# A second attention layer with split keys: one transposed set for both parts of the keys, two copies of the high part, and the maxima one step earlier

## The reference, cut to what matters

```python
ss_g = ss * ms                                   # sigmoid gates, only the 3 largest of 5 kept
sd_g = sd * md
q5 = (x @ Wq).reshape(b, t, H, E, DH)
kv = (x @ Wkv).reshape(b, t, 2, H, E, DH)
k5, v5 = (kv[:, :, 0], kv[:, :, 1])
q = jnp.einsum('bthed,bthe->bhtd', q5, sd_g)
k = jnp.einsum('bthed,bthe->bhtd', k5, ss_g)
v = jnp.einsum('bthed,bthe->bhtd', v5, ss_g)
attn = jax.nn.softmax(jnp.einsum('bhid,bhjd->bhij', q * scale, k), axis=-1)
out = jnp.einsum('bhij,bhjd->bihd', attn, v)
o5 = jnp.einsum('bthd,dm->bthm', out, Wo).reshape(b, t, H, E, DIM)
return jnp.einsum('bthem,bthe->btm', o5, md)
```

## Time and profile before

| | |
|---|---|
| runs | 1804.98 us median of 3 (1800.93 to 1805.13) |
| profiled execution | 1798.95 us, of it span 1797.1 us |
| TensorE matmul | 88% of the span busy |
| VectorE | 72% |
| ScalarE | 53% |
| GpSimd | 41% |
| granted TensorE clock, mean | 0.957 of full speed |

### The profile page before, as it was taken

One profiled execution on the slowest core, in us unless ns is written; L12 is line 12 of the kernel. 1 busy time (PEld: TensorE's weight loads), 2 busy tenths in 40 slices (PEclk: granted clock), 3 DMA queues, 4 the chain that ended last, 5 costly groups with the idle time before them and its releaser, 6 DMA issues.

```text
span 1797.1 us, 26827 instructions
## 1 busy us (share of the span) xinstructions
PE 1582.9 (88%) x8612; PEld 998.3 (56%) x8612; DVE 1292.7 (72%) x2371; ACT 945.1 (53%) x1582; POOL 743.5 (41%) x690
## 2 busy tenths in 40 slices
PE   3799999999999952579999999998999999999997
PEld 2455555555555452556656566565665565665554
DVE  4996785785788357967777777777677777777763
ACT  3456657657555601155655655655656546555552
POOL 2610000000000003647668667488486576685312
PEclk9899999999999975799999999999999999999997
DMA  2000000000000000000000000000000000000000
GB/s 60 1 1 1 1 1 1 1 1 1 1 1 1 1 12 0 12 11 1 1 12 1 5 8 1 12 1 1 12 1 1 12 1 1 1 1 1 1 10 15
DMA packets 12227, 9.38 MB, mean 5 GB/s; under 512 B 3840, under 2 KB 11584, under 8 KB 12096
## 3 DMA queue, kind: packets, MB, share of 16 engines
q1 hardware_dynamic: 12096, 7.66, 1.6%
HBM read 6.61 MB, written 1.05 MB: 4 GB/s over the span
## 4 chain that ended last, share of the span: by engine, by line
PE 64%; POOL 13%; DVE 13%; issue 5%; ACT 3%; SPq 0%; DMA 0%; DVEq 0%; ACTq 0%; POOLq 0%
PE ps L810 10%; PE ps L627 8%; PE ps L644 7%; PE ps L659 7%; POOL z L1432 5%; PE ps L800 4%; PE ps L785 4%; PE ps L801 4%; PE ps L602 4%; POOL onm L1428 3%; PE ps L768 2%; POOL gs L1405 2%; DVE mxp L1111 2%; PE ps L821 2%; PE ps L770 2%
## 5 line engine op out<-in xcount | busy, mean ns | idle before, releaser
L1111 DVE TENSOR_REDUCE mxp<-ps 128x1 f32<-128x512 f32 (+3 forms) x560 | 354.0, 670 | 109.8 <-PE ps L627 55.8
L997 ACT ACTIVATE pbuf<-ps 128x512 f32<-128x512 f32 x512 | 301.5, 598 | 205.5 <-PE ps L801 201.9
L899 ACT ACTIVATE pbuf<-ps 128x1024 f32<-128x1024 f32 (+3 forms) x320 | 281.8, 897 | 197.0 <-PE ps L644 98.0
L1315 DVE TENSOR_TENSOR den<-den,pbuf 128x1024 f32<-128x1024 f32 x224 | 354.1, 1581 | 2.6
L627 PE MATMUL ps<-kM,qT 128*128 128x512 f32 (+3 forms) x640 | 243.1, 425 | 8.9 <-ACT kM L886 4.0
L1268 DVE TENSOR_TENSOR gt<-ps,gate 128x320 f32<-128x320 f32 x384 | 177.3, 484 | 100.8 <-PE ps L770 67.3
L810 PE MATMUL ps<-pbuf,h_v 128*64 128x512 f32 x1024 | 249.7, 608 | 0.0
L1288 DVE CUSTOM_DVE_ANT_0 relu<-ps,relu 128x512 f32<-128x512 f32 x256 | 174.1, 683 | 81.3 <-PE ps L785 78.9
L800 PE MATMUL ps<-q1T,k1T 128*128 128x512 f32 x512 | 212.4, 415 | 10.1 <-ACT pbuf L997 6.2
L644 PE MATMUL ps<-qT,kM 128*128 128x512 f32 (+3 forms) x640 | 207.2, 398 | 8.4 <-ACT pbuf L899 8.4
L983 ACT ACTIVATE relu<-ps 128x512 f32<-128x512 f32 x256 | 151.8, 596 | 107.8 <-PE ps L785 83.6
(11 more groups left out here) (215 smaller groups left out, 2746.3 us busy)
## 6 DMA issues: line engine op xcount, KB each, us to landing
wraw<-in_Wkv SPq DMA_DIRECT2D x16, 160.0 KB, 2.4
wraw<-in_Wq SPq DMA_DIRECT2D x8, 160.0 KB, 2.2
out<-x SPq DMA_DIRECT2D x4, 256.0 KB, 3.1
...
```

The lines of the kernel that those rows point to most:

```text
L899: nc.scalar.activation(pbuf0[:, u % NP0, :, off:CH], ps[:, b:b + 2, off:CH], ACT.Exp, scale=float(D0) ** -0.5).then_inc(s_exp, 1)
L997: nc.scalar.activation(pbuf1[:, u % NP1, i, :], ps[:, i, :], ACT.Exp, scale=float(D1) ** -0.5).then_inc(s_exp1, 1)
L1111: v.tensor_reduce(mxp[:, i, h:h + n, b], ps[:, ring0.bank(step), 0:w * n].rearrange("p (h k) -> p h k", h=n), AX.X, ALU.max).then_inc(s_re ...
L1315: v.tensor_tensor(dn, dn, w, ALU.add).then_inc(s_den1, 1)
```

## The change

1. `hi` writes the high part of the keys once, into columns 0 to 63 of sk1; `lo` writes the low part into columns 64 to 127; sk2 is gone.
2. There are two sets of transposes a chunk instead of three: w=0 turns sk1 (high rows above low rows), w=1 is the queries' set. The w=1 set of the low keys, its turn in the ring of banks and its wait are gone.
3. The copies: from the w=0 bank ScalarE makes three copies of 64 rows (k1T rows 0 to 63, k1T rows 64 to 127 from the same high rows, k2T from the low rows), the last of them releasing the bank; from the queries' bank two as before. Five copies a chunk instead of four.
4. MAX1 is 2.6 instead of 1.6, and q2 stands 2 after m instead of 1: m(c) and all dif and max steps stand one unit earlier, q2(c) stays where it was. The dif and max of chunk 0 have 4.3 units instead of 5.3.

```diff
@@ -53,7 +53,7 @@
 MAX0 = (-1.5, 6.0, 21.0, 44.0)
 PROJ1 = (2.05, 20.5)
 STAGE1 = (2.2, 3.0, 3.7)
-MAX1 = 1.6
+MAX1 = 2.6
 
 
 def preparation0():
@@ -103,7 +103,7 @@
         for c in range(NC):
             end = start + step * TPC * (c + 1)
             out += [(end + STAGE1[0], ("hi", h, c)), (end + STAGE1[1], ("lo", h, c))]
-            out += [(end + STAGE1[2] + 0.3 * w, ("t", h, c, w)) for w in range(3)]
+            out += [(end + STAGE1[2] + 0.3 * w, ("t", h, c, w)) for w in range(2)]
             if c % 2:
                 out.append((end + STAGE1[2] + 0.65, ("kd", h, c // 2)))
         for c in range(NC):
@@ -115,7 +115,7 @@
                 items += [("dif", *b)] if b else []
                 items.append(("max", *a))
             out += [(start + (end - start) * k / len(items), item) for k, item in enumerate(items)]
-            out += [(end, ("m", h, c)), (end + 1, ("q2", h, c))]
+            out += [(end, ("m", h, c)), (end + 2, ("q2", h, c))]
     return sorted(out, key=lambda p: p[0])
 
 
@@ -290,7 +290,6 @@
         mxp1 = s1("mxp1", [P, TPC, NC // 2])
         mx1 = s1("mx1", [P, TPC])
         sk1 = s1("sk1", [P, TPC, P])
-        sk2 = s1("sk2", [P, TPC, D1])
         sq1 = s1("sq1", [P, TPC, P])
         k1T = s1("k1T", [P, 2, T], F32R)
         k2T = s1("k2T", [P, 2, T], F32R)
@@ -771,12 +770,12 @@
                 elif kind == "t":
                     _, h, c, w = step
                     pe.wait_ge(s_st1, NC * h + c + 1)
-                    src = (sk1, sk2, sq1)[w]
-                    chunk_transposes(ring1, step, lambda i: src[:, i, :], D1 if w == 1 else P).then_inc(s_turn1, 1)
+                    src = (sk1, sq1)[w]
+                    chunk_transposes(ring1, step, lambda i: src[:, i, :]).then_inc(s_turn1, 1)
                 elif kind in ("dif", "max"):
                     _, h, it, p = step
                     bank = take(ring1, step)
-                    wait_read(pe, ring1, ("t", h, NC - 1, 2))
+                    wait_read(pe, ring1, ("t", h, NC - 1, 1))
                     if kind == "dif":
                         pe.wait_ge(s_kd, NC // 2 * h + p + 1)
                         keys = kd[:, p, :]
@@ -960,9 +959,8 @@
                     if h == 0:
                         wait_experts(act, TPC * (c + 1) - 2)
                     if h or c:
-                        wait_turn(act, ring1, ("t", h, c - 1, 2) if c else ("t", h - 1, NC - 1, 2))
-                    nc.scalar.activation(sk1[:].rearrange("p n (a d) -> p n a d", a=2).bitcast(F32R),
-                                         h_qk[:, 1, tiles, :].unsqueeze(2).to_broadcast([P, TPC, 2, D1]), ACT.Copy)
+                        wait_turn(act, ring1, ("t", h, c - 1, 1) if c else ("t", h - 1, NC - 1, 1))
+                    nc.scalar.activation(sk1[:, :, 0:D1].bitcast(F32R), h_qk[:, 1, tiles, :], ACT.Copy)
                     nc.scalar.activation(sq1[:, :, 0:D1].bitcast(F32R), h_qk[:, 0, tiles, :],
                                          ACT.Copy).then_inc(s_hi1, 1)
                 elif kind == "t":
@@ -970,11 +968,14 @@
                     wait_turn(act, ring1, step)
                     if h >= 2:
                         act.wait_ge(s_sc1, 2 * U1 * (h - 1))
-                    rows, q = slice(0, D1 if w == 1 else P), slice(CH * c, CH * (c + 1))
-                    if w == 2:
-                        nc.scalar.activation(q2T[0:D1, h % 2, q], ps[0:D1, ring1.bank(step), :], ACT.Copy)
-                    nc.scalar.activation((k1T, k2T, q1T)[w][rows, h % 2, q],
-                                         ps[rows, ring1.bank(step), :], ACT.Copy).then_inc(s_read1a, 1)
+                    q, b = slice(CH * c, CH * (c + 1)), ring1.bank(step)
+                    if w == 0:
+                        nc.scalar.activation(k1T[0:D1, h % 2, q], ps[0:D1, b, :], ACT.Copy)
+                        nc.scalar.activation(k1T[D1:P, h % 2, q], ps[0:D1, b, :], ACT.Copy)
+                        nc.scalar.activation(k2T[0:D1, h % 2, q], ps[D1:P, b, :], ACT.Copy).then_inc(s_read1a, 1)
+                    else:
+                        nc.scalar.activation(q2T[0:D1, h % 2, q], ps[0:D1, b, :], ACT.Copy)
+                        nc.scalar.activation(q1T[:, h % 2, q], ps[:, b, :], ACT.Copy).then_inc(s_read1a, 1)
                 elif kind == "dif":
                     i = SLOT1[step[1:]]
                     wait_turn(act, ring1, step)
@@ -1277,7 +1278,7 @@
                     _, h, c = step
                     tiles = slice(TPC * c, TPC * (c + 1))
                     dve.wait_ge(s_hi1, NC * h + c + 1)
-                    v.tensor_tensor(sk2[:, :, 0:D1], h_qk[:, 1, tiles, :], sk1[:, :, 0:D1], ALU.subtract)
+                    v.tensor_tensor(sk1[:, :, D1:P], h_qk[:, 1, tiles, :], sk1[:, :, 0:D1], ALU.subtract)
                     v.tensor_tensor(sq1[:, :, D1:P], h_qk[:, 0, tiles, :], sq1[:, :, 0:D1],
                                     ALU.subtract).then_inc(s_st1, 1)
                 elif kind == "max":
```

## The result

| | before | after |
|---|---|---|
| median of 18 runs each | 1802.86 us (1798.24 to 1805.13) | 1806.86 us (1805.35 to 1815.06) |
| ratio | | 1.0036, 95% interval 1.0027 to 1.0045 |
| profiled execution, of it span | 1798.95, 1797.1 us | 1813.86, 1812.0 us |
| granted TensorE clock, mean | 0.957 | 0.938 |

What follows compares the result with a forecast made beforehand. A head period was taken as TensorE's work plus some 9 us of stalls; -2.26 us a period, seven times -15.8, with first and last head -18, from 1804.98 to 1787 us, range 1776 to 1800.

Steps and rivals of the forecast that it cites:

- dense sets, c0 and c1: TensorE in c0 and c1: two removed transpose sets of 0.36 us in dense stretches, -0.72 us a period.
- c1, m and a max moved: VectorE in c1: a max and m(c2) leave the stretch ahead of q2(c2), -0.8 us a period, bounds 0 and 0.93.
- c0's proj after q2(c1): c0: m(c1) leaves VectorE's queue ahead of the read TensorE waits for, -0.35 us a period, bounds 0 and 0.5.
- m(c0): c0: m(c0) done some 3 us earlier, TensorE's stall at q2(c0) goes; -0.65 us a period, bounds +0.5 and -1.5.
- c3's extra copy: ScalarE in c3, from hi to the first dif: one more copy at a 0.48 us spacing, +0.48 us a period.
- the gather of c3: GpSimd's last gather, ending at hi(c3): no change counted in the sum, 0 us a period.
- the clock: TensorE's granted clock, read as 1.00 in a head period: no change counted in the sum.
- the gather of c3 comes free: Rival, chance 0.12: denominators fall elsewhere than beside c3's gather, up to 2.8 us a period go; 1773 us.
- It doesn't do what it says: Rival without its own chance: 64-row copies or strided hi dearer than their rows, 0.2 us each, 6 us back, 1793.
- only the dense sets count: Rival, chance 0.17: GpSimd's chain after each F absorbs the maxima's shift; -4 us, up to -9, 1796 to 1801.
- slower: Rival, chance 0.09: in c0 Relus wait for VectorE's max, delaying exponentials and S; 12 us over seven periods, 1817 us.
- The first head: First head's preparation, without scores: 2.3 us go, the extra copy and pairs come back; -1 us.

Runs made afterwards that it cites:

- after filled: After, plus matmuls of unread result in c3, seven ahead of the scores that wait for q2(c3) and five ahead of the first dif: 1799.42 us, ratio 0.9992.
- sets only: After with the maxima back at their old place (MAX1 1.6, q2 one unit after m): 1814.16 us, ratio 1.0069.
- three sets: Before with maxima and q2 one unit earlier and two denominators of c3 moved behind lo(c3), no added matmuls: 1781.33 us, ratio 0.9883.
- maxima only: Before with only the maxima moved (MAX1 2.6, q2 two units after m), its transposes and copies kept: 1815.34 us, ratio 1.0077.
- before, filled: Before, plus matmuls of unread result in c3, one ahead of the scores and three ahead of the first dif: 1802.84 us, ratio 0.9998.
- before, den later: Before with the two denominators between m(c3) and lo(c3) put behind lo(c3) on VectorE: 1799.52 us, ratio 0.9984.

## Why the prediction was wrong, point by point

At full clock (after filled against before), one period, by the terms of the sum:

| term | predicted | measured | from |
|---|---|---|---|
| dense sets, c0 and c1 | -0.72 | -0.7 | sets only: 36.0 for 36.4, 34.44 for 34.75 |
| c1, m and a max moved | -0.8 | -0.5 | after filled 35.5 against sets only 35.9 to 36.0 (with three sets -0.45: 35.92 for 36.37, each at full clock) |
| c0's proj after q2(c1) | -0.35 | +0.27 | maxima only 35.03 for 34.75; after filled 34.71 for sets only 34.44 |
| m(c0) | -0.65 | -0.24 | 11.14 for 10.5, 25.46 for 26.35 |
| hi(c3), half as wide | -0.22 | -0.20 | 3.21 for 3.41 |
| c3's extra copy | +0.48 | +0.84 | 3.95 for 3.12 |
| the gather of c3 | 0 | +0.95 | 11.70 for 10.75 |
| sum | -2.26 | +0.4 | 125.7 for 125.3 |
| the clock | 0 | +1.1 a period in the profiled execution | 852.2 - 844.3 us over seven |

- **Sound**: that a set costs its 0.36 us in the dense stretches and nothing at full clock in c2 and c3, hi's 0.22, and that TensorE's idle time on m(c0) goes: the waits of q2's transposes for L1301 were 15.4 us in the whole trace and are 0.5 for L1302. The place where one period lands was also named: "from onm to the first dif of c3 no shorter than the 16.8 us". It is 18.4 (1255.68 to 1274.04).
- **The step that failed: two costs stood in the sum at nothing**, the gather of c3 (measured +0.95 us a period, 7 us in all) and the clock (8 us over the seven periods, 7 by the medians). The gather first. The rival "the gather of c3 comes free" had the mechanism and even the direction ("one can just as well meet h_qk, which goes undisturbed today"), but only as an argument against a gain. The order of VectorE's instructions behind m(c3) could be read ahead of the run: three den in a row and nothing else until lo. Beside a den each of the gather's instructions takes longer and the reverse (h_qk 1.32 for 0.45), and three den in a row leave none of the four instructions free. It should have stood in the sum at about the 0.87 us by which h_qk grows; with the 0.95 measured the bound of +0.3 us a period for the whole change becomes +1.3, and the -16 us of the seven periods become -9.
- **c3 was priced by durations, not by distances.** For the copies I took one pair that happened to be the cheap kind. A second kind stood in the same rows: the copy of q2(c3) to row 64 starts at 1257.02, and the exponential behind it only at 1257.63. "It doesn't do what it says" asked whether 64-row copies are dearer than their rows. They aren't; their spacing is.
- **The m(c0) term**: the stall goes, but c3's onm to c0's gets only 0.89 us shorter where 1.3 were counted, and 0.65 come back ahead of it, where the two moved matmuls account for 0.48. Whether the Relu chain ate the rest, as the prediction feared, no run tells apart; the middle of the bounds was too good by 0.4.
- **c0's proj after q2(c1)**: its stall grew from 0.78 to 0.91 us instead of shrinking by 0.35. It comes with the maxima alone (0.90 in maxima only, 0.78 in sets only). With m(c1) gone from ahead of it VectorE stands idle 0.28 us before the gt that TensorE waits for, until the gather's h_v (after, 1198.88; no idle time before), so the gather ends the stretch (rival "only the dense sets count", and here it was right); why the wait grows by 0.1 isn't shown.
- **The clock**: I read 1.00 in the earlier trace rows as a property of the layer, but it belonged to a layer with the gaps of before, 0.90 us the longest in c3. The question to ask of every term of c3 was what happens behind a gap of 2 us. The removed set counted as nothing in c3, and yet it widens the gap ahead of the first dif, behind which the clock falls.
- **The range**: its upper end was 1800, although the term by term bounds reached +2 us, 1807, and that bound left out the 2.5 us of the first and the last head which the lower one has in it. The rival "slower" had the right sign by a wrong mechanism: the Relu slots cost little, 7.8 us of waits for exponentials in maxima only against 6.2 before.
- **The first head**: the -1 us can't be read. From the first gather to the first V before has 63.3 us, "before, den later" 65.7 and "before, filled" 67.0, with the same program there, and after 67.1.

By size: of the 2.7 us a period between forecast and outcome at full clock the gather is 0.95, c0's proj 0.6, m(c0) 0.4, the copies 0.36 and c1 0.3. Seven times this, 19 us, and some 7 us of clock by the medians (1806.86 to 1799.42) make 26, where forecast (-18) and result (+4) lie 22 apart. The other 4 stay open. The last head doesn't hold them: from the 28th onm to the last, after filled takes 99.0 us and before 102.1, but before's last stretch ran at 0.92 there; "before, den later", with the same last head at full clock, takes 100.6, so the change gives 1.6 where 1.5 were forecast. Before also has a fall of the clock of its own in one period of its profiled execution (37.9 us for 36.4 in the first column).
